# First attention of a two-layer block: theta from six bf16 products instead of two f32 products, its parts made by ScalarE and GpSimd

## The reference, cut to what matters

```
theta = einsum('ld,bdt->btl', theta_w, ctx) + theta_b      # (8, 512, 128)
phi   = einsum('ld,bdt->blt', phi_w, ln(x)) + phi_b[:, None]
p     = softmax(einsum('btl,bls->bts', theta, phi))
g     = einsum('ld,bdt->btl', g_w, ln(x)) + g_b
t_x   = einsum('bts,bsl->blt', p, g)
h     = relu((t_x - mean) * rsqrt(var + eps) * ln_gamma + ln_beta)
x     = x + (out_w h + out_b) + ctx
```

## Time and profile before

| what | before |
|---|---|
| median of 3 runs (lowest to highest) | 838.62 us (837.96 to 839.0) |
| the profiled execution's own time | 841.42 us |
| span in its trace | 839.7 us |
| TensorE busy | 744.5 us, 89% |
| VectorE busy | 578.2 us, 69% |
| ScalarE busy | 398.3 us, 47% |
| GpSimd busy | 354.9 us, 42% |
| mean granted TensorE clock | 0.951 |

### The profile page before, as it was taken

How to read it: one execution, slowest core, us unless ns; L and a number is a source line. 1 busy time by engine, 2 the same in 40 slices (tenths; PEclk the granted TensorE clock), 3 DMA queues, 4 the chain that set the end, 5 groups by cost and what they waited for, 6 DMA issues and landing times. The chain is left out here.

```text
span 839.7 us, 14278 instructions
## 1 busy us (share of the span) xinstructions
PE 744.5 (89%) x4265; PEld 307.2 (37%) x4265; DVE 578.2 (69%) x1100; ACT 398.3 (47%) x744; POOL 354.9 (42%) x344
## 2 busy tenths in 40 slices
PE   4999997989999999798999899999971699999993
PEld 2344443444444443121222222222231355555551
DVE  4688888585858587668988988976746255555551
ACT  2534543553636372476777667746750222222220
POOL 4654454012020212536576587565465033333332
PEclk9999999999999999799999999968995799999998
DMA  8999740018181775333434453434343589889974
GB/s 307 352 133 257 275 185 0 1 36 303 36 297 71 271 255 183 76 94 84 103 100 103 100 167 94 110 102 119 99 146 142 90 111 131 123 135 120 121 103 62
DMA packets 114166, 117.51 MB, mean 140 GB/s; under 512 B 54824, under 2 KB 78248, under 8 KB 113840
## 3 DMA queue, kind: packets, MB, share of 16 engines
q1 hardware_dynamic: 102992, 94.48, 40.4%
q0 software_dynamic: 10384, 22.02, 15.4%
q10 hardware_dynamic: 720, 0.13, 0.1%
HBM read 43.61 MB, written 59.56 MB: 123 GB/s over the span
## 5 line engine op out<-in xcount | busy, mean ns | idle before, releaser
L1422 ACT ACTIVATE t_room<-l_b 128x512 f32<-128x512 f32 x256 | 139.3, 594 | 53.6 <-PE l_b L1317 47.8
L1930 POOL DMA_INDIRECT out<-ex_y,t_tag x39 | 61.6, 1581 | 123.9 <-DMA out<-ex_y,t_tag 63.7
L1826 PE MATMUL ex_hp<-w1h,h_stack 128*128 x312 | 78.1, 320 | 17.2 <-DVE ex_hl L1879 16.7
L1495 DVE TENSOR_REDUCE l_negm<-l_a 128x2 f32<-128x1024 f32 x64 | 75.2, 1220 | 16.6 <-PE l_a L1262 16.6
L1846 PE MATMUL ex_yp<-w2h,ex_ht 128*128 (+1 forms) x234 | 76.2, 380 | 5.2 <-DVE ex_ht L1890 4.5
L1495 DVE TENSOR_REDUCE h_negm<-l_a 128x2 f32<-128x1024 f32 x56 | 66.0, 1221 | 17.9 <-PE l_a L1262 17.9
L1865 ACT ACTIVATE ex_hf<-ex_pre 128x352 f32<-128x352 f32 x39 | 19.4, 497 | 118.2 <-DVE ex_pre L1885 118.2
L1328 PE MATMUL l_pv<-t_room,l_vt 128*32 128x512 f32 x512 | 73.1, 645 | 0.1
L1336 PE MATMUL l_sm<-t_room,ones_f 128*32 128x512 f32 x512 | 70.3, 623 | 0.0
L806 PE MATMUL ps_st<-f_xt,wg 128*128 128x512 fp8e4 x256 | 65.7, 379 | 3.4 <-ACT f_y L857 1.8
L806 PE MATMUL ps_r<-f_xt,wg 128*128 128x512 fp8e4 x256 | 65.7, 379 | 0.0
(11 more groups left out here) (247 smaller groups left out, 1482.2 us busy)
## 6 DMA issues: line engine op xcount, KB each, us to landing
slots_x<-empty SPq DMA_DIRECT2D x8, 2376.0 KB, 11.1
slots_x<-empty SPq DMA_DIRECT2D x7, 2112.0 KB, 16.1
h_stack<-h_parts SPq DMA_DIRECT2D x96, 64.0 KB
l_stack<-l_parts SPq DMA_DIRECT2D x96, 64.0 KB
f_stage<-in_w SPq DMA_DIRECT2D x8, 704.0 KB, 7.2
w1l<-in_ctx SPq DMA_DIRECT2D x8, 512.0 KB, 8.3
f_stage<-in_w SPq DMA_DIRECT2D x8, 512.0 KB
h_kf<-in_ctx SPq DMA_DIRECT2D x16, 256.0 KB, 3.1
```

Of the source, the lines that this page charges most:

```text
L1422: act.activation(weights_at(u, c, h)[:, :], B[t % 2][:, :], ACT.Exp, scale=SCALE).then_inc(b_ok, 1)
L1495: dve.tensor_reduce(negm[u % 2][:, 2 * half:2 * half + 2, j], A[half][:, :, :], AX.X, ALU.max, negate=True)\
L1826: mm = pe.matmul(HP[i % 2][:, 0:H], xt[i % AHEAD][:, xp * FC + f, :], w1p[wp][:, bass.ds(e, 1), f * H:(f + 1) * H], start=k == 0, stop=k = ...
L1930: pool.indirect_dma_start(out=out, out_offset=bass.IndirectOffsetOnAxis(ap=tags[i % TAGS][:, 0:1].bitcast(U32), axis=0), in_=y[i % YS][:, ...
```

## The change

Theta of batch 0 stays as it was. For batches 1 to 7, `theta_w` gets a high and a low part like the other two weights (`wth` and `wtl` grow from two to three slots), and so does the context: `ch` is made by ScalarE (`high_context`, after `high_x`), `cl` by GpSimd (`low_context`, after `row_rstd`), both for the next batch. TensorE waits for `ch`, makes four bf16 matmuls (high·high and low·high), waits for `cl`, and makes two more.

```
-        wth, wtl = sb("wth", [P, 2, DC, L], BF16), sb("wtl", [P, 2, DC, L], BF16)
+        wth, wtl = sb("wth", [P, 3, DC, L], BF16), sb("wtl", [P, 3, DC, L], BF16)
+        ch = [sb(f"ch{k}", [P, DC, D], BF16) for k in range(2)]
+        cl = [sb(f"cl{k}", [P, DC, D], BF16) for k in range(2)]
...
             def step(i, par, half, now, back, back2, more):
-                pe.wait_ge(ctx_ok[par], 16 * half + 16)
                 wait(pe, g_ok, i)
-                for c in range(DC):
-                    mm = pe.matmul(R[0][:, :], wt[:, 0, c, :], ctxb[par][:, c, :], start=c == 0, stop=c == DC - 1)
+                if isinstance(i, int) and i == 0:
+                    pe.wait_ge(ctx_ok[par], 16)
+                    for c in range(DC):
+                        mm = pe.matmul(R[0][:, :], wt[:, 0, c, :], ctxb[par][:, c, :], start=c == 0, stop=c == DC - 1)
+                else:
+                    pe.wait_ge(ch_ok, i)
+                    k = 0
+                    for wp, cp in ((wth, ch), (wtl, ch), (wth, cl)):
+                        if cp is cl:
+                            pe.wait_ge(cl_ok, i)
+                        for c in range(DC):
+                            mm = pe.matmul(R[0][:, :], wp[:, 0, c, :], cp[par][:, c, :], start=k == 0, stop=k == 3 * DC - 1)
+                            k += 1
                 mm.then_inc(theta_ps, 1)
...
+            def high_context(i, par, half):
+                act.wait_ge(ctx_ok[par], 16 * half + 16)
+                wait(act, theta_ps, i - 1)
+                act.activation(ch[par][:, :, :], ctxb[par][:, :, :], ACT.Copy).then_inc(ch_ok, 1)
...
                 if more:
                     high_x(i + 1, 1 - par)
+                    high_context(i + 1, 1 - par, half + par)
                 if back:
                     biased(act, i)
...
             pool.wait_ge(w_in, 32)
-            pool.tensor_copy(wth[:, :, :, :], wt[:, 1:3, :, :]).then_inc(wth_ok, 1)
+            pool.wait_ge(theta_in, 16)
+            pool.tensor_copy(wth[:, 1:3, :, :], wt[:, 1:3, :, :]).then_inc(wth_ok, 1)
             pool.wait_ge(wth_ok, 1)
-            pool.tensor_tensor(wtl[:, :, :, :], wt[:, 1:3, :, :], wth[:, :, :, :], ALU.subtract).then_inc(wtl_ok, 1)
+            pool.tensor_tensor(wtl[:, 1:3, :, :], wt[:, 1:3, :, :], wth[:, 1:3, :, :], ALU.subtract).then_inc(wtl_ok, 1)
+            pool.tensor_copy(wth[:, 0, :, :], wt[:, 0, :, :]).then_inc(wth_ok, 1)
+            pool.wait_ge(wth_ok, 2)
+            pool.tensor_tensor(wtl[:, 0, :, :], wt[:, 0, :, :], wth[:, 0, :, :], ALU.subtract).then_inc(wtl_ok, 1)
+
+            def low_context(i, par):
+                pool.wait_ge(ch_ok, i)
+                wait(pool, theta_ps, i - 1)
+                pool.tensor_tensor(cl[par][:, :, :], ctxb[par][:, :, :], ch[par][:, :, :], ALU.subtract).then_inc(cl_ok, 1)
...
                 if more:
                     row_rstd(i + 1)
+                    low_context(i + 1, 1 - par)
                 else:
                     G.power(pool, 0)
                 if isinstance(i, int) and i == 1:
                     load_ffn(pool)
```

More of the change, by code:

```diff
@@ L150, in latent_attention @@
         wth_ok, wtl_ok, xh_ok, xl_ok = sem("wth"), sem("wtl"), sem("xh"), sem("xl")
+        ch_ok, cl_ok = sem("ch"), sem("cl")
         theta_ps, phi_ps, g_ps, g_ok = (sem(n) for n in ("thps", "phps", "gps", "gok"))
@@ L238, in chunk_of_g @@
                     for xp, wp in ((xh, wth), (xh, wtl), (xl, wth)):
-                        mm = pe.matmul(R[0][:, s * P:(s + 1) * P], xp[par][:, c, s * P:(s + 1) * P], wp[:, 1, c, :],
+                        mm = pe.matmul(R[0][:, s * P:(s + 1) * P], xp[par][:, c, s * P:(s + 1) * P], wp[:, 2, c, :],
                                        start=k == 0, stop=k == 3 * DC - 1)
@@ L268, in step @@
                     for c in range(DC):
-                        mm = pe.matmul(R[1][:, :], wp[:, 0, c, :], xp[par][:, c, :], start=k == 0, stop=k == 3 * DC - 1)
+                        mm = pe.matmul(R[1][:, :], wp[:, 1, c, :], xp[par][:, c, :], start=k == 0, stop=k == 3 * DC - 1)
                         k += 1
```

## The result

| what | before | after |
|---|---|---|
| median (4 runs each) | 838.29 us (835.95 to 839.0) | 854.84 us (851.65 to 858.34) |
| ratio | | 1.0185, 95% interval 1.0143 to 1.0228 |
| profiled execution, span | 839.7 us | 856.6 us |
| mean granted clock | 0.951 | 0.943 |
| start of the last output product of step 7 (L226, now L229) | 138.88 us | 157.26 us |

The change costs 16.6 us, against a forecast of 12.9 (851.5) with a range of 846.3 to 858.8. The four times after the change are 851.65, 852.13, 857.54 and 858.34 us: no execution took the median, two lie within 0.7 us of the forecast, and the profiled one is the longest. An execution more than 1.5% above the fastest of its kernel counts as slow and enters no median in this document; there was one, of the kernel with filled pauses (862.45 us).

A forecast was written before the change was run, and what follows sets the result against it. It took middle steps to be bound by the mean's wait for bn_aggr, not TensorE's work; 3.04 + 2.24 + 1.7 + 5.95 = 12.9 us on the runs' median of 838.62 gave 851.5 us, range 846.3 to 858.8.

The forecast's parts named there:

- What bounds the step: Middle steps: after phi TensorE idles 0.68 us for bn_aggr before the mean, so a shorter theta only lengthens that wait.
- ScalarE's copy: high_context behind high_x takes 1.05 us; in a middle step theta waits from 72.33 to about 73.35.
- `low_context`: GpSimd's subtraction takes 2.13 us, ending at 75.60 in a middle step; steps 3 to 7 each 1.19 us longer.
- the 0.14 of the hold: Middle step: low_context gets its start at 73.47, is held until 73.61 by L494, and then needs 2.13 less 0.14.
- Rivals 2 and 3: Low part cheap: 847.5, at its lower bound 843.7 (0.09); low part dear, held up 0.5 us more per step: 855.0 (0.05).
- The upper bound of 3.34: Highest time taken as possible for low_context on GpSimd: 2.35 + 0.99 us.
- The mutual hold of GpSimd and VectorE: Each engine waits for the other's running instruction; GpSimd's late addition costs VectorE 1.7 us in step 2, bounds 0 and 2.4.
- The sum: 3.04 (step 1) + 2.24 (step 2) + 1.7 (hold-up in step 2) + 5.95 (steps 3 to 7) = 12.9 us.
- The clock: Rival 1: TensorE's pauses in steps 1 and 2 make its clock fall, 1.8 us each; two falls make 855.1; chance 0.22.
- a clock of 0.5 before 140 us: Sign in the profile after that would show the forecast wrong.
- The faster and the no-change rivals: Faster: TensorE's time decides, 835.7 (0.02). No change: only about 1 us remains, in steps 1 and 2 (0.02).

The follow-up runs named there:

- kernel with filled pauses: The changed kernel with matmuls whose result is overwritten put in TensorE's pauses before the high and low parts; 841.4 us, again 849.8 (+12.3, +14.9 over the kernel before).
- the early parts: The changed kernel with high_context moved right behind phi_h and low_context right behind the addition to X; 832.4 us, +3.2 over the kernel before.
- no low part: The changed kernel without low_context and theta's two matmuls on the low part, the high part kept; 841.8 us, +2.2 over the kernel before.
- low part unused: The changed kernel with four theta matmuls, while GpSimd still makes the low part and nothing waits for it; 847.9 us, +8.3 over the kernel before.
- the kernel with phi first: The changed kernel with TensorE making phi before theta, all parts as in the change; 846.8 us, +17.6 over the kernel before.

## Why the prediction was right, and where it was off

*What bounds the step.* Right. The mean's wait for `bn_aggr` takes any time that theta gives back: the early parts show it at its purest, 0.68 to 1.11.

*ScalarE's copy.* Right in place and size (0.95 and 2.67 us of waiting). Without the low part it costs nothing in middle steps.

*`low_context`.* Taken as 2.13. It is 2.12 to 2.14 where VectorE's `low_x` isn't beside it (the early parts) and 2.22 in the change. The working took the 0.14 of the hold off its time after having waited for it, though a held operation does its work later (L601 with its 0.99). That it came out even so (TensorE's fifth matmul starts 2.22 us after the first, forecast 2.30) is because `low_context` started 0.18 earlier against theta than forecast. The middle step is 18.34 against 18.36, and 18.2 to 18.3 in the filled kernel. Against the steps before, of 16.99 to 17.17, that is 1.2 to 1.3 longer, for 1.19. Rivals 2 and 3 fall with it. The upper bound of 3.34 was needlessly far.

*The mutual hold of GpSimd and VectorE.* Right, with the sizes foreseen: 1.6 for 1.7 in step 2. By the Trainium skill ("SBUF — State Buffer", "SBUF: two separate sides") whichever of the two engines starts first keeps the port pair that they share for its whole instruction, and an operation of the other that needs the pair is blocked; the casts of 1.85 and 1.25 us that end with GpSimd's addition agree. So already L515, a cast with one input, was held, where the working had stressed the two inputs of L517. I had charged it only in step 2. It is the floor beneath the middle steps as well: with TensorE's wait taken away the steps don't return to 16.99 to 17.17 but to 17.83 to 17.89. The wait adds 1.2 to 1.3 to a step and hides this second cost of 0.7 to 0.85; they don't add.

*The sum.* 12.9 against 13.3 and 13.7 at the end of the attention in the two profiles without falls. Its parts hold as well: steps 1 and 2 together 7.2 and 7.5 for 6.98, the later ones 6.2 both times for 5.95.

*The clock: the step that failed.* The prediction took the falls as a rival at 0.22, confined to steps 1 and 2, on the ground that "pauses of 1.0 and 1.4 us in the middle steps speak against it". Three profiles of the change have the clock fall in steps 1 and 2 each time, and in one to three of the middle ones. So by a sign that the prediction itself had named, a clock of 0.5 before 140 us, it was wrong here. Pauses of 0.95 and 1.19 us with 0.87 of work between came before a fall in five of fifteen middle steps; where the 1.19 was gone (no low part, low part unused), none of ten had a fall. A fall in a middle step costs 1.5 to 1.7 us (19.85 for 18.30 in step 3, 19.92 for 18.24 in step 6, against the filled kernel), for 1.8 foreseen. In step 1 it costs 0.5 to 2.8 (18.14 to 20.45 for 17.65). It was also wrong to add it to the hold-up of step 2: there the fall delays VectorE until GpSimd is done, the cast takes 0.17, and the fall and the hold-up together cost 0.1 to 1.2 us more than the hold-up alone (19.97 to 21.10 for 19.91). So the likeliest case was the forecast's mechanism with three to five falls, and the measured 854.84 lies 3.3 above the forecast, near the 855.1 of the rival, but through more falls than it had, at other prices. That the median lies so well inside the range is in part luck: in the profiled execution the attention alone took 18.4 us more, 5.5 over the sum, and the rest of the kernel gave 1.5 back.

*The faster and the no-change rivals* had 0.04 between them, and no run lends them anything.

## What to carry to other kernels

Before making a matmul cheaper, look at what the next instruction on that engine waits for; if it waits for something that the matmul doesn't feed, the saving goes into that wait first (here all of the 0.42 us), and any operand that must now be made first comes on top. When work goes to GpSimd, look for VectorE instructions that fall into its long operations: the loss shows as tiny instructions that last a microsecond, in a list by duration and not in a list of waits. Two costs on different engines at the same place in a step were a maximum here, not a sum, so undoing one showed only the difference to the next.

## What was not expected of the hardware

A cast of 128x4 on VectorE took up to 2.27 us (in the kernel with phi first) and a subtraction of 128x4 2.26 us, both 0.17 otherwise, and an operation on one column 2.12 for 0.22, while GpSimd worked. And the granted clock of TensorE fell to near 0.5 in steps whose longest pause was 1.19 us, where in the kernel before pauses of 1.20 us (step 0) and 2.14 us (at 178 us) had passed without a fall; the trace doesn't say which of such steps it will be, and that stays open.
